# Experts: gate and up ahead of the transposes on TensorE, weight copies ahead of the transposed rows on ScalarE

## What is computed

```python
x = x + _L0_xattn_ref(_layernorm(x), ctx, ...)
x = x + _L0_ffn_ref(_layernorm(x), ...)   # silu(x @ w1.T) * (x @ w3.T) @ w2.T, weighted, 16 experts, top 2
x = x + _L1_xattn_ref(_layernorm(x), ctx, mask, ...)
x = x + _L1_ffn_ref(_layernorm(x), ...)   # 32 experts, top 4:
#   gate = min(x @ w_gate + b_gate, 7); up = clip(x @ w_up + b_up, -7, 7)
#   out = ((up + 1) * gate * sigmoid(1.702 * gate)) @ w_down + b_down
```

## Time and profile before

| | us |
|---|---|
| median of 3 runs | 1792.15 |
| lowest and highest | 1791.57 and 1800.09 |
| span of the profiled execution | 1784.9 |
| experts of layer 0, in the span | about 928 to 1075 |
| experts of layer 1, in the span | about 1440 to 1717 |

### The profile page before, as it was taken

The page is one execution under the profiler, slowest core; times in us unless marked ns, Lnnn a source line. Parts: engine busy times, 40 slices in busy tenths (PEclk is TensorE's granted clock), DMA queues, the critical chain, the costliest instruction groups (busy, mean ns, idle before and its releaser), DMA issues.

```text
span 1784.9 us, 43889 instructions
## 1 busy us (share of the span) xinstructions
PE 1540.2 (86%) x14968; PEld 1241.0 (70%) x14968; DVE 1333.0 (75%) x2901; ACT 1071.7 (60%) x3276; POOL 1093.7 (61%) x1111
## 2 busy tenths in 40 slices
PE   4999999999999999989977773998895179999966
PEld 3888888888888888866646661565563169898955
DVE  3899889999998899976624443698887248787876
ACT  3888888888888888844324432665651045555510
POOL 2766767667667676646735565547776736566642
PEclk9999999999999999989989886999996579999989
DMA  6500000000000000022244435102222945454447
GB/s 181 175 19 20 19 20 11 20 20 20 19 19 20 19 20 19 8 84 79 85 144 142 147 108 188 48 29 97 79 74 99 324 142 161 154 162 151 154 188 285
DMA packets 103080, 167.65 MB, mean 94 GB/s; under 512 B 20223, under 2 KB 75980, under 8 KB 102480
## 3 DMA queue, kind: packets, MB, share of 16 engines
q1 hardware_dynamic: 77136, 105.37, 19.0%
q0 software_dynamic: 22272, 56.15, 8.6%
q10 hardware_dynamic: 3456, 3.34, 0.6%
HBM read 95.31 MB, written 75.76 MB: 96 GB/s over the span
## 4 chain that ended last, share of the span: by engine, by line
PE 66%; issue 11%; DVE 9%; POOL 5%; another core or an unknown queue 2%; DMA 2%; SPq 1%; ACT 1%; ACTq 0%; DVEq 0%; POOLq 0%
PE layers_banks L323 14%; PE layers_banks L297 13%; PE layers_banks L309 9%; PE layers_banks L877 7%; PE layers_banks L888 4%; PE layers_banks L1250 3%; PE layers_banks L282 3%; PE layers_banks L286 3%; PE layers_banks L865 2%; POOL l_by_token L991 2%; PE layers_banks L1263 1%; DVE weights L1843 1%; PE layers_banks L2128 1%; PE layers_banks L1610 1%
## 5 line engine op out<-in xcount | busy, mean ns | idle before, releaser
L461 POOL TENSOR_TENSOR w_down<-w_down,layers_arena 128x1024 f32<-128x1024 f32 x256 | 483.5, 1893 | 234.9 <-DVE layers_arena L420 234.0
L387 ACT ACTIVATE w_down<-layers_banks,layers_arena 128x256 f32<-128x256 f32 x1024 | 468.7, 498 | 1.8 <-DVE layers_arena L414 1.8
L991 POOL DMA_INDIRECT l_by_token<-layers_arena x240 | 245.7, 1024 | 194.2 <-issue 100.7
L425 DVE COPY w_down<-layers_banks 128x1024 f32<-128x1024 f32 x256 | 312.0, 1219 | 40.6 <-PE layers_banks L309 37.1
L414 DVE TENSOR_REDUCE layers_arena<-layers_banks 128x4 f32<-128x1024 f32 x256 | 309.4, 1209 | 41.0 <-PE layers_banks L297 40.6
L297 PE MATMUL layers_banks<-layers_arena 64*128 64x256 f32 x2048 | 279.7, 385 | 2.9 <-ACT w_down L387 2.2
L323 PE MATMUL layers_banks<-w_down,layers_arena 128*64 128x256 f32 x2048 | 250.6, 386 | 1.6 <-DVE w_down L425 1.3
L387 ACT ACTIVATION_READ_ACCUMULATOR w_down<-layers_banks,layers_arena 128x1 f32 x1024 | 237.9, 232 | 0.0
L877 PE MATMUL layers_banks<-layers_arena 128*128 128x128 f32 x1600 | 207.9, 283 | 25.1 <-ACT layers_arena L915 18.0
L1160 POOL DMA_INDIRECT l_rows_in<-layers_arena,l_routing_group_slots x192 | 189.7, 988 | 57.7 <-issue 44.9
L309 PEld LDWEIGHTS layers_banks<-ident,w_down 64*128 64x128 f32 x4096 | 168.7, 138 | 78.0 <-issue 72.0
(11 more groups left out here) (225 smaller groups left out, 2508.4 us busy)
## 6 DMA issues: line engine op xcount, KB each, us to landing
layers_arena<-l_rows_in SPq DMA_DIRECT2D x240, 136.0 KB
weights<-l_by_token SPq DMA_DIRECT2D x32, 512.0 KB, 9.7
layers_arena<-in_ctx SPq DMA_DIRECT2D x64, 128.0 KB, 2.8
layers_arena<-l_by_token SPq DMA_DIRECT2D x32, 256.0 KB, 2.7
weights<-in_w_gu SPq DMA_DIRECT2D x16, 512.0 KB
l_rows_in<-zeros SPq DMA_DIRECT2D x1, 4352.0 KB
x_sb<-in_x SPq DMA_DIRECT2D x32, 128.0 KB
w_down<-in_w_down SPq DMA_DIRECT2D x1, 4096.0 KB
```

Source lines behind the costliest of these rows:

```text
L387: last = nc.scalar.activation(prob[:, n % 4, c, :], ps_s[:, n % 2, c, :], ACT.Exp, bias=negmax[:, n % 2, c:c + 1], accum_out=sums[:, n % 2 ...
L425: nc.vector.tensor_copy(prob_t[:, n // 2 % 2, n % 2, :, :, :].rearrange("p k c (d s) -> p d (k c) s", d=2), ps_t[:, :, :, :].rearrange("p ...
L461: nc.gpsimd.tensor_tensor(prob[:, n % 4, :, :], prob[:, n % 4, :, :], rsum[:, n % 2, :].unsqueeze(2).to_broadcast([P, 4, A_N]), ALU.mult). ...
L991: pool.indirect_dma_start(m.by_token, bass.IndirectOffsetOnAxis(ap=place, axis=0), outs[:, r % RING, b, :], None, bounds_check=T * m.K - 1 ...
```

## The change

Only `experts` is touched, on two engines. On PE, `gate_up` of pair r + 1 stands ahead of `transposes` of pair r + 2. On ACT, a step begins with the weight copies of r + 2; in layer 0 (no bias) the function of r + 1 follows and then the row copy of r + 2, in layer 1 the row copy and then the function. The waits of each piece are the same as before, and so are all instructions and their number; DVE, POOL and SP are unchanged.

```diff
         def step(it, r):
+            if exists(it, r + 1):
+                gate_up(it, r + 1)
             if exists(it, r + 2):
                 transposes(it, r + 2)
-            if exists(it, r + 1):
-                gate_up(it, r + 1)
             if exists(it, r - 1):
                 down(it, r - 1)
...
         def step(it, r):
             if exists(it, r + 2):
-                q = r + 2
-                done(act, x_made, it, q)
-                done(act, gu_made, it, q - 2)
-                nc.scalar.activation(rows_t[:, q % 2, :, :, :], ps_x[:, q % 2, :, :, :], ACT.Copy).then_inc(x_ready, 1)
+                weights_of(r + 2)
+            if bias is None and exists(it, r + 1):
+                function(r + 1)
             if exists(it, r + 2):
...
+                transposed(r + 2)
+            if bias is not None and exists(it, r + 1):
+                function(r + 1)
```

More of the change, by code:

```diff
@@ L904, in _, with transposed, weights_of @@
         experts_of = block_experts(mybir.EngineType.Activation)
+        def transposed(q):
+            done(act, x_made, 0, q)
+            done(act, gu_made, 0, q - 2)
+            nc.scalar.activation(rows_t[:, q % 2, :, :, :], ps_x[:, q % 2, :, :, :], ACT.Copy).then_inc(x_ready, 1)
+        def weights_of(q):
+            e = experts_of(0, q)
+            done(act, gu_made, 0, q - 2)
+            for b in range(2):
+                last = nc.scalar.activation(w_now[:, q % 2, b, :, :].rearrange("p k n -> p (k n)"),
+                                            w_gu[:, bass.ds(e[b], 1), :, :].rearrange("p a k n -> p (a k n)"), ACT.Copy)
+            last.then_inc(w_ready, 1)
@@ L906, in step, with function @@
+        def function(q):
+            done(act, a_ready, 0, q - 2)
+            if bias is None:
+                done(act, gu_made, 0, q)
+                nc.scalar.activation(glu[I:P, q % 2, :, :], ps_gu[0:I, q % 2, 0, :, :], ACT.Silu).then_inc(function_ready, 1)
+            else:
+                done(act, gate_ready, 0, q)
+                nc.scalar.activation(glu[:, q % 2, :, :], gate[:, q % 2, :, :], ACT.Sigmoid, scale=ALPHA)\
+                    .then_inc(function_ready, 1)
         def step(it, r):
```

## The result

The changed kernel is slower: 1816.61 us (median of 4 runs, 1807.57 to 1819.69) against 1794.11 (median of 4, 1791.57 to 1800.09), a ratio of 1.0118 with a 95% interval of 1.0092 to 1.0144. The time lies in the range of the prediction, but on the side of its slow rival (1809 us), not at the forecast of no change (1797). The profiled execution has a span of 1814.8 us and took 1816.6 in all, so only 1.8 us lie around a span.

What follows compares the result with a forecast made beforehand. It took layer 0 as bound by rounds of unbroken GpSimd stores with late TensorE signals, layer 1 by a VectorE-GpSimd ring. Span 1784.9 + 4.4 (layer 1 +2.4, layer 0 +2, ends 0) + 7.3 = 1796.6, forecast 1797 us, range 1774 to 1820.

Steps and rivals of the forecast that it cites:

- slow rival: Layer 0: row copy behind a waiting function, TensorE dry a pair earlier, four-pair rounds of 16.1 us; 1809 us, chance 0.33.
- the ring of gate_up, transposes, copy and gate_up: Layer 1: new order closes this chain in one step, 3.12 us a pair against TensorE's own 3.09 and the present 3.27.
- the term of +2.4 us: Layer 1: cost of the closed chain, the full 0.03 us for all 80 pairs.
- Weight copies first: Layer 1: their 1.15 us run while TensorE is in gate_up, 1.79 us; costed at nothing.
- The likeliest case: Whole kernel: no change a measurement could tell, 1797 us, own range 1788 to 1801; chance 0.42.
- the chain of 2.22 us: Layer 0: gate_up to down 0.89, then 0.63, copy 0.60 and signal 0.10; under the stores' 2.58 a pair, so not felt.
- the round of 10.49 us: Layer 0: unbroken stores 7.43, late signal 1.33, next store 1.73 us; three pairs, 3.50 us a pair, taken as the bound.
- 0.77 a pair: Layer 1 bound: extra us if the transposes' signal is late by 0.92 with 0.15 to spare; up to 62 us.
- about zero together: Ends of both stages: first pair's copies no longer ahead of gate_up (-1.15), second pair's transposes wait (at most +1.79 us).
- The +2 us put on layer 0: Layer 0: allowance for rounds that begin with one more wait, the row copy queuing behind the function.
- The fast rival: Layer 0: TensorE paces GpSimd, breaks let signals through, about 2.8 us a pair, 21 us less, 1776 us; chance 0.18.
- 7.3 us: Whole kernel: time around the 1784.9 us span up to the 1792.15 us median, added unchanged to the forecast.

Runs made afterwards that it cites:

- e7: Kernel before, plus a 0.56 us GpSimd write to an unused buffer behind each pair's two stores in layer 0: 1788.93 us, ratio 0.9949.
- e12: Kernel before, plus a GpSimd write of 0.99 us behind each pair's two stores in layer 0: 1790.91 us, ratio to before 1.0017.
- e6: Changed kernel, plus a 0.56 us GpSimd write to an unused buffer behind each pair's two stores in layer 0: 1793.46 us, ratio to before 0.9985.
- e13: Kernel before, plus a 0.56 us GpSimd write between the two stores of each pair in layer 0: 1780.13 us, ratio to before 0.995.
- e1: Changed kernel with ScalarE's layer 0 function behind the row copy again, the rest kept: 1806.11 us, ratio to before 1.0077.
- e4: Kernel before with the whole change in layer 1 alone, layer 0 as before: 1794.11 us, ratio 1.0002.
- e8: Changed kernel with ScalarE's layer 1 weight copies behind the row copy again: 1876.98 us in one run.
- e2: Changed kernel with TensorE's old order (transposes ahead of gate_up), ScalarE's new order kept: 1798.0 us, ratio to before 1.0029.
- e10: Kernel before, plus a 0.56 us GpSimd write behind each pair's stores in both layers: 1788.9 us, ratio 0.9968.
- e9: Changed kernel, transposes and row copy one pair further ahead, plus a 0.56 us GpSimd write behind each pair's stores, both layers: 1796.74 us, ratio to before 1.0.

## Why the prediction came out as it did

**The reading of the profile** held. Layer 0 is bound by rounds in which TensorE's signals are held while GpSimd stores without a break; e7 and e12 show it: with breaks between the stores the held waits halve or vanish. In e6 and e13 signals are still held, but GpSimd hardly runs dry. In layer 1 the ring of gate_up, transposes, copy and gate_up closes as the prediction put it together:

```profile
1591.81 0.60 PE L865 MATMUL layers_banks<-ident,layers_arena 128*128 128x128 f32 x4
...
1592.44 0.60 ACT L909 ACTIVATE layers_arena<-layers_banks 128x512 f32<-128x512 f32 x1 [1.27 <-PE layers_banks L865]
...
1593.19 2.02 PE L877 MATMUL layers_banks<-layers_arena 128*128 128x128 f32 x16
...
1595.05 0.60 PE L865 MATMUL layers_banks<-ident,layers_arena 128*128 128x128 f32 x4
```

1593.19 - 1592.44 = 0.75 for copy and signal (0.60 + 0.15), 1.86 to the next transposes, 0.63 to their copy: 3.24 us, in 59 of 79 steps. The prediction's 3.12 was too low by 0.07 in gate_up and 0.05 in the copy's signal. The rest of layer 1's 262.5 us are five single steps, 6.7 us together, each like this one, where stores had come to follow each other and the transposes' signal was held:

```profile
1669.52 0.60 PE L865 MATMUL layers_banks<-ident,layers_arena 128*128 128x128 f32 x4
1669.56 0.99 POOL L1000 DMA_INDIRECT l_by_token<-layers_arena  x1 [0.30 <-DVE layers_arena L976]
...
1672.05 0.60 ACT L909 ACTIVATE layers_arena<-layers_banks 128x512 f32<-128x512 f32 x1 [3.20 <-issue]
```

So the term of +2.4 us was right as far as can be told. The +4.0 between the two profiled executions is less than the spread of the old order's layer 1 (258.5 to 266.0 us), the new order's is 260.0 to 262.5 in e1, e4, e6 and the changed kernel, and e4's total is within half a per cent of nothing.

**Weight copies first**, costed at nothing: right, with the cover that was named, and e8 shows its price.

**The likeliest case failed in layer 0**, at the sentence that the chain of 2.22 us is "not felt while the round of 10.49 us stands". The chain was priced with a transposes signal that arrives at once, 0.63 from start to copy, a row of layer 1. In the same stage I had read off that TensorE's signals are held by more than a microsecond, and for layer 1 I had put that case into the bounds (0.77 a pair). In layer 0 I left it out. With it the chain that the new order closes in one step has a hold in it, and the rounds lose the down that had been TensorE's reserve: 13.6 us between the first store and the last. The ends of the stage failed too. They were put at "about zero together", but ahead of the first store no round covers the chain, TensorE was at its lower level there, and the chain took 3.68 us a pair: 4.4 us more before the first store. The +2 us put on layer 0 should have been +18; that is 0.48 us a pair, over the 0.2 at which the prediction called itself wrong.

**The slow rival** had the outcome: TensorE dry one pair earlier, rounds of four pairs, 16.1 us predicted when cold and 15.1 to 15.9 measured, the gate_up or down behind each release at half speed, the clock under 0.88. By the rule of "HAM oscillation" in the Trainium skill's page "TensorE: Matmul & The Clock Gate", with every round cold, its term for layer 0 was 21 us. The trace agrees with the rule as far as each round of the late part of the stage has matmuls at half speed (1.91 us for a down above, 2.05 for a gate_up in e1). The rival itself had 15 us for layer 0, and 18.6 were measured. Its reason was wrong, though: it put the late copy down to the function ahead of it on ScalarE. e1 and e2 show that ScalarE's order is not it; the copy is late because the transposes' signal is. That its number came so near is therefore luck in part, the more so as 4.4 of the 18.6 us lie at the start of the stage, which no rival had; and that the time fell into the stated range is owed to this rival.

**The fast rival**, a round that breaks because TensorE paces GpSimd, came about only in passing: from 959.54 to 968.77 us of the changed kernel the stores go in pairs 3.0 to 3.2 us apart, with breaks of 0.7 to 0.9 us, and no wait is "remote"; then the rounds are back. What it said of breaks is true in e7. Its sum has a slip: 1792 - 21 + 2.4 is 1773, not 1776, which has the 2 us for layer 0 in it as well.

**Around the span** I carried 7.3 us over. It is 1.8; the rest was that the profiled execution of before was quicker than the median run. This made no difference to the sum, but hid that the execution from which all rows came was not a middle one.

## What to carry to other kernels

When a trace shows that one engine's signals arrive late, price every signal of that engine as late, in each chain that a reordering closes, above all one that used to have a whole step to spare. An order that lets a producer's work run a step earlier than needed is a reserve against late signals even where no wait shows it. And where GpSimd issues indirect stores back to back beside a dependent TensorE loop, try a short break between them: more work on the engine that sets the pace can shorten the stage. It did so here in layer 0; in layer 1 of the kernel before it changed nothing (e10).

## What the runs showed of the hardware

TensorE's signals to ScalarE and VectorE come late while GpSimd issues indirect stores that follow each other at 0.30 us. They do not do so from the first store on: in the six stores from 1023.01 us of the changed kernel, a gate_up that ended 1.5 us after the first one's start was answered 0.1 us later (1024.60), the next, which ended 3.9 us after it, 3.4 us later (1030.29). In layer 0 of the two kernels the held weighs and row copies start 0.9 to 1.4 us after the end of the last store; some functions start while it still runs, as that of 1030.29 does (1029.46 to 1030.44). Signals of transposes, gate_up and down are held alike and come out 0.06 us apart (e1); TensorE itself goes on with its next instructions meanwhile.

The signals do not wait for the last store's data: the weigh held until 969.81 in the kernel before starts 1.0 us after the end of the store at 967.81, but 0.9 us ahead of the events by which that store's data land (970.74 to 970.99). A break of 0.7 us between stores halves weigh's held time in layer 0 of the kernel before, takes it only from 34.8 to 30.1 us in the changed one, and does not shorten the row copy's in layer 1 (e9); one of 1.1 us (e12) leaves no held wait in layer 0. What in GpSimd or behind it holds the signals, no run here shows.
